# Experts stage: TensorE reads the last 24 row tiles' weight numbers two at a time in twelve steps instead of eight at a time in three

## The chip, the cores and the metric

The kernel runs on one core of one Trainium2 chip. The metric is the device time of the program in microseconds (us), the median of several runs. A core has TensorE (PE in the profile; its weight loads are shown apart, as PEld), VectorE (DVE), ScalarE (ACT), GpSimd (POOL) and SyncE (SP). Each has its own instruction queue, and TensorE's is read by a sequencer that also carries out its waits and register instructions; these are called PEq or PEldq in the profile.

## What is computed

Two blocks of a small transformer, on x of 8 x 1024 rows of 256 numbers. Only the first block's expert part touches the change:

```
xn = layernorm(x)
expert_idx = argmax(xn @ gate_w.T)                 # 8 experts, one for each row
g, u  = xn @ wg[expert], xn @ wu[expert]           # 256 -> 64 each
inter = square(relu(g)) * u
out   = inter @ wd[expert]                         # 64 -> 256
x = x + linear_attention(xn) * silu(out)
xn = layernorm(x)
x = x + block_attention(xn) * silu(layernorm(xn + heads(xn)) * ln_g + ln_b)
```

The kernel leaves out the term `heads(xn)`, the reference's head-wise attention over chosen rows, in both versions; nothing of the second block is touched.

## The kernel before, in words

The program has three parts that follow one another on each engine: `first_layer`, `experts` and `second_layer`. Here only `experts` (from line 1038) matters.

**Sorting.** The first layer scatters the normalised rows into a DRAM table that is sorted by expert. They are then read back as row tiles of 128 rows, each belonging to one expert. There are 72 slots for such tiles (`SLOTS`), worked on in 36 pairs (`PAIRS`), the last with one tile. Which rows stand at which slot is known only at run time: VectorE writes two tables into SBUF, `row_i` (where each tile starts in DRAM) and `owners_i` (the number of the expert whose weights each tile needs, the tile's weight number).

**Registers.** TensorE's matmuls of a tile choose their weights by such a number, which must be in a register of TensorE. It has 48 registers `owners` for this (`OWNERS`), filled by `load_owners` (lines 1210 and 1211), one `TENSOR_LOAD` instruction for eight neighbouring numbers. Six of these loads fill all 48 registers ahead of the stage, between the matmuls of the first layer's last values (`values`, line 1244, with `owners_from`; `whole_values`, line 181, calls `between`). The other 24 numbers follow during the stage, when the first registers are free again: the table `OWNER_LOADS` (line 1047) says in which step.

**The steps.** TensorE's part of the stage is `step(m)` (line 1216), m from 0 to 37, written out without a loop on the chip. In program order a step in the middle of the stage holds:

- `gate_up(m)`: 4 matmuls, `gu_ps`, line 1183, for each a register instruction ahead that works out the address of the weights;
- where `m in OWNER_LOADS`: the load of owners, line 1211;
- `turn_hidden(m - 1)`: 2 transposes, `ht_ps`, line 1193; its first wait is line 1191's, a wait instruction of its own;
- `down(m - 2)`: 4 matmuls, `y_ps`, line 1202, again with a register instruction each;
- `turn(m + 3)`: 4 transposes, `t_ps`, line 1159.

Other engines work on the pairs beside this: ScalarE and VectorE between the matmuls, SP and POOL issue the DMAs that read the row tiles (`load_again`; their own registers `row` are filled from `row_i` by `load_rows`, line 1093, eight at a time) and SP stores `y` to the DRAM tensor `expert_rows`. At the end of the stage POOL waits for all stores (`stored`, ahead of line 1991) and gathers the rows back for the second layer (line 1972).

Before the sorted order is known in full, SP and POOL each take four tile starts one at a time from the same table (`tile_start`, line 223).

Of the kernel before, what the change touches and what calls it, by code (L numbers as in the profile page):

```python
# [39 lines left out]
def program(nc, x, W, gate_w, wg, wu, wd, W_qkv, W_out, b_out, ln_g, ln_b, out):  # L40
# [16 lines left out]
    with ExitStack() as whole:  # L57
# [54 lines left out]
        z.eps_bias = sb("eps_bias", [P, z.D])  # L112
        z.turned = z.wdn[:].rearrange("p e d -> p (e d)").rearrange("p (f k n) -> p f k n", f=4, k=z.KD)
        moe = experts(nc, z, W_qkv, W_out, b_out, ln_g, ln_b)
        second = second_layer(nc, z)
        block = whole.enter_context(nc.Block())
# [64 lines left out]
def whole_values(nc, pe, z, p, banks, free, between=None):  # L181

    v = ORDER[p]
    slot = WHOLE_ROWS.index(v // ROW)
    pe.wait_ge(z.kv_split, WHOLE_ROWS[slot] + 1)
    pe.wait_ge(z.rows_ready, z.UT * free)
    for t in range(z.UT):
        for j in range(z.KD):
            m = nc.tensor.matmul(banks[:, t, 0:z.NV], parked(z, v)[:, j, t * P:(t + 1) * P], z.kvf[:, slot, j, :], start=(j == 0), stop=(j == z.KD - 1))
            if between and j == 0:  # L190
                between(t)
    m.then_inc(z.v_ready, 1)
# [843 lines left out]
def experts(nc, z, W_qkv, W_out, b_out, ln_g, ln_b):  # L1036

    KD, D, E, DE, SLOTS = z.KD, z.D, z.E, z.DE, z.SLOTS
    QUAD = 4
# [3 lines left out]
    PAIRS = SLOTS // 2  # L1043
    ROUNDS = PAIRS // QUAD
    OWNERS, OCTET = 48, 8
    STORE_LAG = 2 * QUAD + 1
    OWNER_LOADS = {14: 48, 17: 56, 20: 64}
    WEIGHT_TURNS = {PAIRS - 3 + f: (f,) for f in range(4)}
    assert PAIRS == ROUNDS * QUAD and OWNERS + OCTET * len(OWNER_LOADS) == SLOTS
    assert z.B * z.L % P == 0  # L1050

    def width(n):

        return 1 if isinstance(n, int) and n == PAIRS - 1 else 2

    with ExitStack() as ctx:
# [90 lines left out]
        def tensor(pe):  # L1147
            def turn(n, i, reused):
                for u in range(2):

                    pe.wait_ge(loaded[u][i], (n - i) * (16 // QUAD) + 16)
                if reused:
                    pe.wait_ge(g["t_copied"], n - 1)
                else:
                    pe.wait_ge(z.first_sems["kv_ready"], ROWS)
                    pe.wait_ge(z.kv_split, ROWS)
                for k in range(KD):
                    for u in range(width(n)):
                        t = nc.tensor.transpose(t_ps[:, i % 2, k, u, :], xg[:, i, u, k * P:(k + 1) * P], z.ident[:])  # L1159
                t.then_inc(g["t_ready"], 1)  # L1160

            def turn_weight(f):

                if f == 0:
                    pe.wait_ge(g["w2_centred"], 3)
                if f < 2:
                    pe.wait_ge(g["t_copied"], PAIRS - 1 + f)
                else:
                    pe.wait_ge(z.turned_copied, f - 1)
                src = z.w2[:, :, f * D:(f + 1) * D] if f < 3 else z.wo[:]  # L1170
                o = t_ps[:, f % 2].rearrange("p k u t -> p k (u t)")
                for k in range(KD):
                    for j in range(KD):
                        t = nc.tensor.transpose(o[:, k, j * P:(j + 1) * P], src[:, j, k * P:(k + 1) * P], z.ident[:])
                t.then_inc(z.turned_ready, 1)

            def gate_up(n, i, e, reused):
                pe.wait_ge(g["t_copied"], n + 1)
                if reused:
                    pe.wait_ge(g["hid_ready"], n - 1)  # L1180
                for u in range(width(n)):
                    for k in range(KD):
                        m = nc.tensor.matmul(gu_ps[:, i % 2, u * 2 * DE:(u + 1) * 2 * DE], xgt[:, i, k, u, :],  # L1183
                                             z.wgu[:, k, bass.ds(e[u], 1), :].rearrange("p a f -> p (a f)"),
                                             start=(u == 0 and k == 0), stop=(k == KD - 1), skip_group_check=True)
                m.then_inc(g["gu_ready"], 1)

            def turn_hidden(n, i, reused):
                pe.wait_ge(g["hid_ready"], n + 1)
                if reused:  # L1190
                    pe.wait_ge(g["ht_copied"], n - 1)
                for u in range(width(n)):
                    t = nc.tensor.transpose(ht_ps[:, i % 2, u * P:(u + 1) * P], hid[:, i % 2, u].rearrange("p c f -> p (c f)"), z.ident[:])
                t.then_inc(g["ht_ready"], 1)

            def down(n, i, e, reused):
                pe.wait_ge(g["ht_copied"], n + 1)
                if reused:
                    pe.wait_ge(g["silu_ready"], n - 1)
                for u in range(width(n)):  # L1200
                    for part in range(2):
                        m = nc.tensor.matmul(y_ps[:, i % 2, u, :], hidt[:, i % 2, u, :],  # L1202
                                             wdn2[:, part, bass.ds(e[u], 1), :].rearrange("p a h -> p (a h)"),
                                             start=(u == 0 and part == 0), stop=(part == 1), skip_group_check=True)
                m.then_inc(g["y_ready"], 1)

            owners = [pe.alloc_register(f"owner{j}") for j in range(OWNERS)]

            def load_owners(first):  # L1210
                pe.load(owners[first % OWNERS:first % OWNERS + OCTET], z.owners_i[0:1, first:first + OCTET])

            def experts_of(n):
                return [pe.snap(owners[(2 * n + u) % OWNERS], min_val=0, max_val=E - 1) for u in range(width(n))]

            def step(m):
                if m < PAIRS:
                    if m == 0:

                        pe.wait_ge(z.rows_ready, z.UT * (START[2] + 1))  # L1220
                    gate_up(m, m % QUAD, experts_of(m), m >= 2)
                if m in OWNER_LOADS:
                    load_owners(OWNER_LOADS[m])
                if m == 0:
                    turn(2, 2, True)
                    values(START[4], START[1])
                    turn(3, 3, True)
                if 1 <= m <= PAIRS:
                    if m == 1:

                        pe.wait_ge(z.rows_ready, z.UT * (START[4] + 1))
                    turn_hidden(m - 1, (m - 1) % QUAD, m - 1 >= 2)
                if m >= 2:
                    if m == 2:

                        pe.wait_ge(z.rows_ready, z.UT * (START[3] + 1))
                        pe.wait_ge(g["wdn_split"], 1)
                    down(m - 2, (m - 2) % QUAD, experts_of(m - 2), m - 2 >= 2)
                if m > 0 and m + 3 < PAIRS:
                    turn(m + 3, (m + 3) % QUAD, True)  # L1240
                for f in WEIGHT_TURNS.get(m, ()):
                    turn_weight(f)

            def values(p, before, owners_from=None):

                load = owners_from is not None and (lambda t: load_owners(owners_from + t * OCTET))
                whole_values(nc, pe, z, p, value_banks[p], before + 1, load)

            values(START[0], TAIL[0])
            pe.wait_ge(z.first_sems["tables_made"], 2)  # L1250
            values(START[1], TAIL[1], 0)
            values(START[2], TAIL[2], 2 * OCTET)
            values(START[3], START[0], 4 * OCTET)
            for i in range(2):
                turn(i, i, False)
            for m in range(PAIRS + 2):
                step(m)
# [785 lines left out]
```

## Time and profile before

| | |
|---|---|
| median of 3 runs | 509.13 us (508.62 to 509.9) |
| profiled execution, its own time | 508.11 us |
| profiled execution, its span | 506.2 us |
| TensorE busy (matmuls) | 494.1 us, 98% of the span |
| VectorE, ScalarE, GpSimd busy | 452.2, 396.5, 320.4 us |
| share of PE in the chain that ended last | 89% |
| loads of owners during the stage | 3, of eight numbers each, at 246.8, 253.5 and 260.2 us |

Times inside a trace count from the span's start. The profiled execution took 1.9 us more than its span; that is what lies before the first and behind the last instruction. Two matmuls that follow one another overlap in the trace, so the pace of TensorE is read from starts, not from durations. Rows for PEldq are instructions that TensorE's sequencer carries out itself; they are not counted as busy time. The step numbers of the stage are found by counting the groups of eight `gu_ps` records: step 14 begins at 246.46 us.

### The profile page before, as it was taken

Reading aid. Unit: us, or ns where it says so; the run is one execution under the profiler, and the core shown is the slowest. Engines: PE = TensorE matmul, PEld = TensorE weight load, DVE = VectorE, ACT = ScalarE, POOL = GpSimd, SP = SyncE. Lnnn points to the kernel's source line nnn. Section 1 sums busy time; section 2 is a strip of 40 time slices with the busy share of each in tenths; the row PEclk is TensorE's granted clock in tenths of the full one; section 3 lists DMA queues with packets and bytes.
Section 4 is the critical chain, followed back from the end, with each engine's and each line's share of the span. In section 5 each row is a group of like instructions: output and inputs, shape, how many; then the busy total and the mean of one; then the engine's idle time right before and its main releaser. Section 6 shows DMA issues by size and latency. Waiting matters only on the chain.

```text
span 506.2 us, 11940 instructions
## 1 busy us (share of the span) xinstructions
PE 494.1 (98%) x3599; PEld 462.9 (91%) x3599; DVE 452.2 (89%) x1428; ACT 396.5 (78%) x910; POOL 320.4 (63%) x377
## 2 busy tenths in 40 slices
PE   6999999999999999999999999999999999999996
PEld 5999999999999999899999998888888898888885
DVE  6999999999999988969889949999999999999975
ACT  4878878787878784378888866788888888888885
POOL 5568876767676877454553028777877777877300
PEclk9999999999999999999999999999999999999999
DMA  7942322222222114558878563265665555655511
GB/s 221 258 126 86 124 84 84 85 84 84 85 85 84 43 53 167 160 170 246 249 231 260 180 206 119 69 145 128 139 147 126 141 131 132 142 139 126 105 42 64
DMA packets 59303, 67.70 MB, mean 134 GB/s; under 512 B 11880, under 2 KB 53616, under 8 KB 59248
## 3 DMA queue, kind: packets, MB, share of 16 engines
q1 hardware_dynamic: 44304, 38.69, 25.5%
q0 software_dynamic: 14944, 28.32, 22.4%
q8 instruction: 29, 0.48, 0.4%
q14 instruction: 26, 0.21, 0.2%
HBM read 39.85 MB, written 27.13 MB: 132 GB/s over the span
## 4 chain that ended last, share of the span: by engine, by line
PE 89%; POOL 3%; DVE 3%; DMA 2%; issue 2%; ACT 1%; SPq 0%; DVEq 0%; POOLq 0%
PE v_ps L1548 10%; PE q_ps L1526 10%; PE gu_ps L1183 6%; PE s_ps L1568 5%; PE y_ps L1202 3%; PE k_ps L171 3%; PE m_ps L171 3%; PE tq_ps L171 3%; PE m_ps L173 3%; PE m_ps L172 3%; PE k_ps L172 3%; PE t_ps L1159 3%; PE k_ps L173 3%; PE tq_ps L172 3%; PE tq_ps L173 3%; PE tq_ps L418 3%
## 5 line engine op out<-in xcount | busy, mean ns | idle before, releaser
L1972 POOL DMA_INDIRECT four<-expert_rows,gather_u x64 | 69.1, 1079 | 37.3 <-DMA expert_rows<-y 18.6
L978 POOL DMA_INDIRECT sorted_rows<-xn,row_u x64 | 67.6, 1057 | 17.2 <-issue 14.1
L967 POOL TENSOR_TENSOR xn<-xn 128x512 fp32r<-128x512 f32 x32 | 43.2, 1350 | 29.6 <-ACT xn L581 29.3
L1526 PE MATMUL q_ps<-xt,wqk 128*128 128x256 f32 x256 | 60.6, 379 | 0.0
L1548 PE MATMUL v_ps<-wvo,xt 128*128 128x256 f32 x248 | 58.7, 379 | 0.0
L1526 PEld LDWEIGHTS q_ps<-xt,wqk 128*128 128x128 f32 x256 | 48.5, 190 | 6.9 <-issue 0.4
L1548 PEld LDWEIGHTS v_ps<-wvo,xt 128*128 128x128 f32 x248 | 44.8, 190 | 4.8
L1978 POOL DMA_DIRECT2D res<-in_L_attn_x x26 | 34.9, 1341 | 19.0 <-DVE res L1775 17.3
L227 POOL DMA_DIRECT2D four<-sorted_rows x36 | 20.0, 555 | 39.8 <-PE t_ps L1159 35.0
L1688 ACT ACTIVATE xn2nd<-res,shift,rstd 128x256 f32<-128x256 f32 (+1 forms) x64 | 34.7, 594 | 7.9 <-DVE shift L1819 7.8
L171 PE MATMUL tq_ps<-xt,wq 128*128 128x256 f32 x128 | 38.4, 300 | 1.9 <-DVE xt L717 1.9
L1987 POOL TENSOR_TENSOR rstd<-var_eps,neg_half 128x4 f32<-128x4 f32 x32 | 35.4, 1106 | 7.7 <-DVE var_eps L1811 7.6
L571 ACT ACTIVATE xn<-four,shift,rstd 128x255 f32<-128x255 f32 x64 | 34.9, 600 | 6.2 <-POOL shift L961 6.2
L609 ACT ACTIVATE k<-kf 128x512 fp32r<-128x512 f32 x32 | 20.2, 630 | 23.7 <-DVE kf L730 23.7
L1183 PE MATMUL gu_ps<-wgu,xgt 128*128 x284 | 37.7, 275 | 0.3 <-ACT xgt L1266 0.3
L171 PE MATMUL k_ps<-wkg,xt 128*128 128x264 f32 x128 | 37.7, 294 | 0.0
L171 PE MATMUL m_ps<-k,xn 128*128 128x256 f32 x128 | 36.2, 283 | 0.4 <-DVE k L736 0.4
L172 PE MATMUL k_ps<-wkg,xt 128*128 128x264 f32 x128 | 36.4, 284 | 0.0
L173 PE MATMUL k_ps<-wkg,xt 128*128 128x264 f32 x128 | 36.3, 283 | 0.0
L173 PE MATMUL m_ps<-k,xn 128*128 128x256 f32 x128 | 36.1, 282 | 0.0
L172 PE MATMUL m_ps<-k,xn 128*128 128x256 f32 x128 | 36.1, 282 | 0.0
L172 PE MATMUL tq_ps<-xt,wq 128*128 128x256 f32 x128 | 35.7, 279 | 0.0
(292 smaller groups left out, 1791.9 us busy)
## 6 DMA issues: line engine op xcount, KB each, us to landing
expert_rows<-y SPq DMA_DIRECT2D x35, 256.0 KB, 3.4
four<-in_L_attn_x SPq DMA_DIRECT2D x32, 256.0 KB, 3.0
out_rows<-att SPq DMA_DIRECT2D x31, 256.0 KB, 2.1
res<-in_L_attn_x POOLq DMA_DIRECT2D x26, 256.0 KB, 4.9
four<-sorted_rows SPq DMA_DIRECT2D x36, 128.0 KB, 3.6
four<-sorted_rows POOLq DMA_DIRECT2D x36, 128.0 KB, 3.3
wdn<-in_L_ffn_wd SPq DMA_DIRECT2D x2, 512.0 KB, 6.8
sorted_rows<-res SPq DMA_DIRECT2D x8, 128.0 KB, 5.7
```

What stands on the lines that cost most here:

```text
L171: nc.tensor.matmul(out, lhs[0], rhs[0], start=first, stop=False, **kw)
L172: nc.tensor.matmul(out, lhs[0], rhs[1], start=False, stop=False, **kw)
L173: return nc.tensor.matmul(out, lhs[1], rhs[0], start=False, stop=last, **kw)
L571: m = nc.scalar.activation(xn[:, i, t, 0:D - 1], xa[:, i % X_SLOTS, t, 0:D - 1], ACT.Identity, bias=shift[:, i % X_SLOTS, t:t + 1], scale= ...
L967: nc.gpsimd.tensor_tensor(xn2[:, s, 1], xn[:, i], xn2[:, s, 0].bitcast(F32), ALU.subtract).then_inc(g["xn_split"], 1)
L978: nc.gpsimd.indirect_dma_start(out=z.sorted_dram.ap(), out_offset=bass.IndirectOffsetOnAxis(ap=row_u[:, i // CU, k:k + 1], axis=0), in_=xn ...
L1183: m = nc.tensor.matmul(gu_ps[:, i % 2, u * 2 * DE:(u + 1) * 2 * DE], xgt[:, i, k, u, :], z.wgu[:, k, bass.ds(e[u], 1), :].rearrange("p a f ...
L1526: m = nc.tensor.matmul(q_ps[:, j, :], wqk[:, k, j * P:(j + 1) * P], xt[:, i % 2, k, :], start=(j == 0 and k == 0), stop=(k == KD - 1), ski ...
L1548: m = nc.tensor.matmul(v_ps[:, t, :], xt[:, i % 2, k, t * P:(t + 1) * P], wvo[:, k, :], start=(t == 0 and k == 0), stop=(k == KD - 1), ski ...
L1972: nc.gpsimd.indirect_dma_start(out=moe[:, n % SLOTS, t, :], out_offset=None, in_=z.expert_dram.ap()[0:(z.SLOTS - 1) * P, :], in_offset=bas ...
L1978: nc.gpsimd.dma_start(tiles(n), x_units[n], accum_op=ALU.add).then_inc(x_added[n % SLOTS], 16)
L1987: nc.gpsimd.tensor_tensor(rstd[:, s], var_eps[:, s], z.neg_half[:, 0:2 * UT].rearrange("p (a t) -> p a t", a=2), ALU.pow).then_inc(g["rstd ...
```

## The change

`OWNER_LOADS` gets twelve entries instead of three: in each of the steps 10 to 21, TensorE reads the weight numbers of one pair of tiles (48 and 49 in step 10, 50 and 51 in step 11, and so on to 70 and 71 in step 21). The six loads of eight ahead of the stage stay as they are.

```diff
     OWNERS, OCTET = 48, 8
     STORE_LAG = 2 * QUAD + 1
-    OWNER_LOADS = {14: 48, 17: 56, 20: 64}
+    OWNER_LOADS = {10 + k: OWNERS + 2 * k for k in range((SLOTS - OWNERS) // 2)}
...
-            def load_owners(first):
-                pe.load(owners[first % OWNERS:first % OWNERS + OCTET], z.owners_i[0:1, first:first + OCTET])
+            def load_owners(first, count):
+                pe.load(owners[first % OWNERS:first % OWNERS + count], z.owners_i[0:1, first:first + count])
...
                 if m in OWNER_LOADS:
-                    load_owners(OWNER_LOADS[m])
+                    load_owners(OWNER_LOADS[m], 2)
...
-                load = owners_from is not None and (lambda t: load_owners(owners_from + t * OCTET))
+                load = owners_from is not None and (lambda t: load_owners(owners_from + t * OCTET, OCTET))
```

TensorE's program in step 10, before the change, from the register instructions of `gate_up` on (ISA is a register instruction, x2 a row that repeats):

```order
L1183 ISA
L1183 MATMUL gu_ps<-wgu,xgt 128x128
L1193 MATMUL ht_ps<-ident,hid 128x128 x2
L1214 ISA
L1202 ISA
```

The same place with the change:

```order
L1183 ISA
L1183 MATMUL gu_ps<-wgu,xgt 128x128
L1211 TENSOR_LOAD owners_i
L1193 MATMUL ht_ps<-ident,hid 128x128 x2
L1214 ISA
L1202 ISA
```

A load stands now between the last matmul of `gate_up` and the first transpose of `turn_hidden`. It stands at the same place in steps 11 to 21; in steps 14, 17 and 20 it stood there before, too. TensorE's program grows by nine instructions, from three loads in the stage to twelve; nothing else on it changes its order, and the programs of the other four engines are the same row for row.

## Rows read from the trace of the kernel before

**Rows 1.** The page, parts 1 and 2: busy time of each engine, TensorE's granted clock

```profile
PE 494.1 (98%) x3599; PEld 462.9 (91%) x3599; DVE 452.2 (89%) x1428; ACT 396.5 (78%) x910; POOL 320.4 (63%) x377
...
PEclk9999999999999999999999999999999999999999
```

**Rows 2.** Timeline of PE: start us, us, engine, line, operation [idle before]

```profile
244.44 1.06 PE L1183 MATMUL gu_ps<-wgu,xgt 128*128 x8
...
246.46 1.06 PE L1183 MATMUL gu_ps<-wgu,xgt 128*128 x8
248.04 0.41 PE L1193 MATMUL ht_ps<-ident,hid 128*128 128x128 f32 x2 [0.53 <-issue]
...
249.44 1.06 PE L1183 MATMUL gu_ps<-wgu,xgt 128*128 x8
...
251.46 1.06 PE L1183 MATMUL gu_ps<-wgu,xgt 128*128 x8
...
253.48 1.06 PE L1183 MATMUL gu_ps<-wgu,xgt 128*128 x8
254.78 0.41 PE L1193 MATMUL ht_ps<-ident,hid 128*128 128x128 f32 x2 [0.24 <-issue]
...
256.13 1.06 PE L1183 MATMUL gu_ps<-wgu,xgt 128*128 x8
...
260.17 1.06 PE L1183 MATMUL gu_ps<-wgu,xgt 128*128 x8
261.47 0.41 PE L1193 MATMUL ht_ps<-ident,hid 128*128 128x128 f32 x2 [0.24 <-issue]
...
262.90 1.06 PE L1183 MATMUL gu_ps<-wgu,xgt 128*128 x8
```

**Rows 3.** TensorE's loads (duration ns min/median/max, starts us): ahead of the stage, then in it

```profile
L1211 PEldq TENSOR_LOAD <-owners_i x6: 588/598/778, 208.6 to 213.1; - x6
...
L1211 PEldq TENSOR_LOAD <-owners_i x3: 1103/1124/1146, 246.8 to 260.2; - x3
```

**Rows 4.** Other engines' loads, the same view: one number each (L223), eight each (L1093)

```profile
L223 SPq TENSOR_LOAD <-row_i x4: 268/316/528, 205.6 to 207.7; - x4
L223 POOLq TENSOR_LOAD <-row_i x4: 286/331/542, 205.6 to 207.7; - x4
...
L1093 POOLq TENSOR_LOAD <-row_i x8: 566/673/906, 211.0 to 271.8; - x8
L1093 SPq TENSOR_LOAD <-row_i x8: 521/536/549, 212.7 to 272.7; - x8
```

**Rows 5.** The wait instruction behind each load and that of the next step: starts

```profile
L1191 PEldq EVENT_SEMAPHORE  x2: 51/51/51, 247.9 to 249.7; - x2
...
L1191 PEldq EVENT_SEMAPHORE  x2: 51/51/51, 254.7 to 256.3; - x2
...
L1191 PEldq EVENT_SEMAPHORE  x2: 51/51/51, 261.4 to 263.1; - x2
```

**Rows 6.** The chain that ended last, 288 to 330 us: start us, us, what

```profile
293.35 0.86 PE y_ps L1202 x4
...
296.08 2.03 DMA expert_rows<-y
...
299.03 1.03 POOL four L1972
...
317.56 3.19 DMA four<-expert_rows,gather_u
...
325.85 0.66 PE t_ps L1539 x4
```

**Rows 7.** Waits, 293 to 330 us: who waited for whom, us, times, longest

```profile
POOL four L1972 <- DMA expert_rows<-y: 18.6, 1, 18.6
```

**Rows 8.** Window of step 14: PE, PEld, DVE, ACT, POOL busy, PEclk, DMA share, GB/s

```profile
246.46:249.44 2.98, 2.45 (x21) 2.15 (x19) 2.61 (x7) 1.99 (x6) 1.21 (x2) 1.00 0.88 233
```

More of the change, by code:

```diff
@@ L1046, in experts @@
     STORE_LAG = 2 * QUAD + 1
-    OWNER_LOADS = {14: 48, 17: 56, 20: 64}
+    OWNER_LOADS = {10 + k: OWNERS + 2 * k for k in range((SLOTS - OWNERS) // 2)}
     WEIGHT_TURNS = {PAIRS - 3 + f: (f,) for f in range(4)}
-    assert PAIRS == ROUNDS * QUAD and OWNERS + OCTET * len(OWNER_LOADS) == SLOTS
+    assert PAIRS == ROUNDS * QUAD and OWNERS + 2 * len(OWNER_LOADS) == SLOTS
     assert z.B * z.L % P == 0
```

## The prediction

> **What bounds the kernel now.** I began with the page's busy times and clock. TensorE is busy for 98% of the span, and its granted clock is in the top tenth in all 40 slices [rows 1]; so what counts is time in which TensorE starts nothing. Next the timeline of TensorE in the experts stage. A step is read from one group of `gu_ps` starts to the next: 244.44 to 246.46, 2.02 us, and the same from 249.44 to 251.46 and on to 253.48 [rows 2]. With no idle time beside it, 2.02 us is the array's own pace. Three steps are longer, and they are the three with a load: 2.98 us (246.46 to 249.44), 2.65 (253.48 to 256.13) and 2.73 (260.17 to 262.90), each with an idle gap ahead of `ht_ps` that is put down to issue [rows 2]. So the three loads cost 0.96 + 0.63 + 0.71 = 2.30 us now, 0.77 each.
>
> Then I asked the loads themselves. Eight numbers took TensorE 0.59 us ahead of the stage, but 1.10 to 1.15 in it, 1.12 in the middle [rows 3]. The sequencer is held that long, while the array works off what was queued before; what the queue does not cover is lost. Last I looked at whether a loss here reaches the end. The chain runs from the last `y_ps` at 293.35 over the store of `y` and POOL's gathers to the second layer's first transposes at 325.85 [rows 6], and POOL had stood waiting for that store for 18.6 us [rows 7]. Nothing in this chain is early, so I pass TensorE's delay on in full.
>
> **The change, part by part.** It removes three loads of eight, puts twelve loads of two in steps 10 to 21, and moves nothing else. Registers are free in time: those that step 10 refills were last used in step 2 and are next read in step 24. SP's, POOL's, ScalarE's and VectorE's programs are the same, and no wait is added; behind the load in TensorE's queue stand `turn_hidden`, `down` and `turn`, and behind these their readers, which all shift with it.
>
> *Removed:* 2.30 us, if all three losses go.
>
> *How long a load of two takes.* No row shows one on TensorE, so I bound it. On SP one number took 0.268 us at least and eight 0.521 at least; on POOL 0.286 and 0.566 [rows 4]. That is (0.521 - 0.268) / 7 = 0.036 us for each further number, 0.040 on POOL. A load is mostly a fixed cost: six numbers fewer save 6 x 0.036 = 0.22 us. Ahead of the stage a load of two would so take 0.59 - 0.22 = 0.37. What doubles the load in the stage (1.12 against 0.59, 0.53 more) the trace doesn't say. SP's loads of eight in the same stage don't show it (0.521 to 0.549), POOL's now and then do (up to 0.906) [rows 4]; it is thus the engine's own doing, not the memory's. The least it can be with two numbers is nothing (0.37), the most that nothing shrinks (1.12). I take a fixed 0.53, since it hardly varies over the three loads, though the first of them came when less was queued (it lost 0.96 where the others lost 0.63 and 0.71): 1.12 - 0.22 = **0.91 us**.
>
> *How fast the sequencer is.* This decides, since twelve loads follow one another, one a step. Behind each of the three loads the array had caught up, and the sequencer ran as fast as it can: from the wait of line 1191 to that of the next step took 249.7 - 247.9 = 1.8, 256.3 - 254.7 = 1.6 and 263.1 - 261.4 = 1.7 us [rows 5], 1.70 in the mean. From a load's end to that wait pass some 0.05 us (260.2 + 1.15 against 261.4 [rows 3, 5]). So a step with no load leaves the sequencer 2.02 - 1.70 = 0.32 us to get ahead, and a step with a load of duration d needs 1.75 + d of sequencer time. With d = 0.91 that is 2.66 us: **0.64 us more than the array's 2.02, in each step**, with nothing to recover it in between.
>
> *The sum.* The first of the twelve meets a sequencer that is ahead, as the three do now: 0.77 - 0.22 = 0.55. The other eleven: 11 x 0.64 = 7.04. Together 7.6 lost, 2.30 given back: **+5.3 us**. The profiled execution took 508.11 us, so 513.4 for one like it; it lay 1.0 us below the median of the three runs (509.13), so I predict a median of **514.4**. The pace of 1.70 is known to about 0.1, which is 1.1 us over eleven steps: 513.3 to 515.5 if the mechanism holds.
>
> For any d the same sum reads: (d - 0.35) + 11 x (d - 0.27) - 2.30. It is zero at d = 0.47. Every rival below but the last is this line with another d.
>
> The Trainium skill, in "DMA: Bandwidth & Descriptors", section "Latency and other measured facts", gives a `tensor_load` floor of about 600 ns. SP's loads of one in 0.268 us [rows 4] lie below that, so the trace speaks against it for SP; it would speak against this change, and no row here tests it for TensorE with fewer than eight.
>
> **The rivals.**
>
> 1. *The count does not matter on TensorE.* Then d = 1.12: 0.77 + 11 x 0.85 - 2.30 = +7.8, 516.9. For it: the cost is mainly fixed on the two other engines. Against it: on both, eight took about twice as long as one [rows 4]. This is where the skill's floor would lead, with the stage's extra on top.
> 2. *The whole load shrinks by one factor.* d = 1.12 / 0.59 x 0.37 = 0.70: 0.35 + 11 x 0.43 - 2.30 = +2.8, 511.9.
> 3. *The stage's extra is a price for each register written.* Then two carry a quarter of it: d = 0.37 + 0.13 = 0.50, 0.15 + 11 x 0.23 - 2.30 = +0.4, 509.5. For it: SP doesn't show the extra, and TensorE alone has register-addressed matmuls queued when it loads. Against it: no row shows such a price.
> 4. *Not slower: short loads hide.* If the extra is gone with so short a load, d = 0.37, and a step needs 1.75 + 0.37 = 2.12 us of the sequencer, 0.10 over the array. 0.02 + 11 x 0.10 - 2.30 = -1.2, 507.9. This decides from d = 0.47 downwards; below 0.34 the gain is over 1.5 us, and it ends at -2.3 (506.8), where all is hidden. For it: six of nine loads on TensorE show no extra. Against it: these six had no register instructions around them, and the three in the stage all show it. The Trainium skill, in "Runtime: NRT & Kernel Launch", section "Instruction fetch mechanics", puts a register load at some 200 ns a register; by that two would take 0.4 and the sum would be -0.8, but eight would take 1.6, and the trace has 0.59 and 1.12 [rows 3].
> **How the numbers follow.** The forecast has 0.47 (513.3 to 515.5), rival 1 0.17, rival 2 0.12, rival 3 0.10, rival 4 0.10, rival 5 0.01; the rest, 0.03, is what I have not thought of. The range goes from rival 4's 507.9 to a little over rival 1's 516.9: 507.8 to 517.2. The cases inside it hold over 0.9, but leaving either out would drop a bound of the unknown duration. A measurement of this kernel tells a change from none at about 0.3%, 1.5 us. Slower by more than that are the forecast and rivals 1, 2 and 5, 0.77 in all, of which I give 0.02 back for a pace of the sequencer that I read too slow: 0.75. Within are rival 3 and most of rival 4: 0.18. Faster by more than 1.5 us, d under 0.34: 0.07.
>
> **What the profile of the changed kernel would show.** Twelve loads in the stage, one in each of steps 10 to 21, of 0.85 to 0.95 us. `gu_ps` groups that start 2.6 to 2.75 us apart from step 11 on, with an idle gap of about 0.4 us put down to issue ahead of every `ht_ps`, and 2.02 again from step 22. The wait of line 1191 comes 1.75 us plus a load behind the one before. The last `y_ps` of the stage and the second layer's first transposes both come 5 us later, and behind 330 us nothing is longer than before. I am wrong if a load of two takes under 0.6 or over 1.05 us, if the steps with loads stay near 2.02, or if TensorE's delay at 293 us isn't found again at 326.

## The result, and the profile after

Measured side by side on one chip, the change takes 512.92 us (median of 4 runs, 512.62 to 513.2) and the kernel before 509.51 (4 runs, 508.62 to 510.06): a ratio of 1.0066, 95% interval 1.0048 to 1.0083. It is slower by 3.4 us, 2.4 to 4.2 by the interval. The profiled execution took 513.1 us, its span 511.2.

Busy time and granted clock, parts 1 and 2 of the page of the changed kernel, to set against [rows 1]:

```profile
PE 499.0 (98%) x3599; PEld 465.4 (91%) x3599; DVE 452.9 (89%) x1428; ACT 396.5 (78%) x910; POOL 320.8 (63%) x377
...
PEclk9899999999999999999999999999999999999999
```

PE's busy time grew by 4.9 us with the same 3599 matmuls, and the others' stayed. Most of that lies in the changed steps. Windows over steps 10 to 21, before and after (us; PE, PEld, DVE, ACT, POOL busy; PEclk, DMA share, GB/s):

```profile
238.37:264.92 26.55, 25.54 (x219) 24.60 (x217) 22.56 (x53) 23.16 (x60) 14.31 (x19) 1.00 0.82 243
...
240.44:269.72 29.28, 28.86 (x219) 25.50 (x217) 23.11 (x54) 23.67 (x60) 14.69 (x19) 1.00 0.77 223
```

The twelve steps take 2.73 us more, and TensorE is recorded as busy for 3.3 us more, so the loss doesn't look like idle time. Without a load, `ht_ps` starts 0.89 us behind `gu_ps`, whose group of records lasts 1.06: the two overlap. With a load it starts 1.04 us behind, the overlap is gone, and the lost time counts as busy. A busy share can't show this loss; starts can.

The clock's second slice is a tenth lower. It lies over 200 us ahead of the first changed instruction and is not the change's. The changed kernel's stage also began late in this execution, ahead of any changed instruction; whether the clock is the reason isn't shown, but it has to be taken off first. First and last starts of three kinds of matmul (duration ns min/median/max, first and last start us), in the kernel before:

```profile
L1159 PE MATMUL t_ps<-ident,four x142: 270/272/274, 214.4 to 286.8; 128*128 128x128 f32 x142
L1202 PE MATMUL y_ps<-wdn,hidt x142: 277/284/384, 222.4 to 294.6; 128*128 x142
L1539 PE MATMUL t_ps<-ident,xn2nd x128: 272/274/328, 310.9 to 491.0; 128*128 128x128 f32 x64, 128*127 128x128 f32 x64
```

The same rows of the changed kernel:

```profile
L1159 PE MATMUL t_ps<-ident,four x142: 270/272/329, 216.3 to 291.6; 128*128 128x128 f32 x142
L1202 PE MATMUL y_ps<-wdn,hidt x142: 277/288/388, 224.3 to 299.4; 128*128 x142
L1539 PE MATMUL t_ps<-ident,xn2nd x128: 272/274/329, 316.9 to 496.0; 128*128 128x128 f32 x64, 128*127 128x128 f32 x64
```

The stage began 1.9 us late (216.3 against 214.4) and ended 4.8 us late (299.4 against 294.6). So the stage itself gave 2.9 us, and the last transpose of the second layer is 5.0 us late, as the span is. The group that started at 325.85 in the chain of [rows 6] is 5.25 us late (timeline of PE of the changed kernel):

```profile
331.10 0.65 PE L1539 MATMUL t_ps<-ident,xn2nd 128*128 128x128 f32 x4
```

Between the two parts the lateness is not constant: the second layer's very first transposes are 6.0 us late (316.9 against 310.9). The wait that [rows 7] showed for the store of `y` is unchanged, in the waits of GpSimd (who waited for whom, us, times, longest):

```profile
POOL four L1972 <- DMA expert_rows<-y: 18.5, 1, 18.5
```

TensorE's steps, timeline of PE of the changed kernel (start us, us):

```profile
238.29 1.06 PE L1183 MATMUL gu_ps<-wgu,xgt 128*128 x8
...
240.44 1.06 PE L1183 MATMUL gu_ps<-wgu,xgt 128*128 x8
241.48 0.41 PE L1193 MATMUL ht_ps<-ident,hid 128*128 128x128 f32 x2
...
242.83 1.06 PE L1183 MATMUL gu_ps<-wgu,xgt 128*128 x8
244.03 0.41 PE L1193 MATMUL ht_ps<-ident,hid 128*128 128x128 f32 x2
...
245.40 1.06 PE L1183 MATMUL gu_ps<-wgu,xgt 128*128 x8
...
269.72 1.06 PE L1183 MATMUL gu_ps<-wgu,xgt 128*128 x8
270.61 0.38 PE L1193 MATMUL ht_ps<-ident,hid 128*128 128x128 f32 x2
...
271.74 1.06 PE L1183 MATMUL gu_ps<-wgu,xgt 128*128 x8
```

Step 10 starts at 240.44, step 22 at 269.72: 29.28 us for twelve steps, 2.44 each, where the array's own pace is 24.24 (12 x 2.02). In the kernel before, the same twelve took 26.55. From step 22 on it is 2.02 again (269.72 to 271.74). `ht_ps` starts 1.04 and 1.20 us behind `gu_ps` in the first two steps with a load, 0.89 in the first without.

TensorE's loads in the stage, then the first three alone, then the wait of line 1191 over steps 10 to 21 (same columns as above), of the changed kernel:

```profile
L1211 PEldq TENSOR_LOAD <-owners_i x12: 533/628/818, 240.7 to 267.5; - x12
...
L1211 PEldq TENSOR_LOAD <-owners_i x1: 590/590/590, 240.7 to 240.7; - x1
...
L1211 PEldq TENSOR_LOAD <-owners_i x1: 818/818/818, 243.0 to 243.0; - x1
...
L1211 PEldq TENSOR_LOAD <-owners_i x1: 550/550/550, 245.6 to 245.6; - x1
...
L1191 PEldq EVENT_SEMAPHORE  x12: 51/51/51, 241.4 to 268.2; - x12
```

The twelve loads have a mean of 0.654 us, against the 1.12 of [rows 3]. The waits come (268.2 - 241.4) / 11 = 2.44 us apart; less 0.65 that leaves 1.78, where I had 1.75. The later kernels with a load in every step give the same: 2.33 us between loads less a mean of 0.54 is 1.79 in twos_turn, 2.31 less a mean of 0.51 is 1.80 in ones24.

### The profile page after: what moved, and what is told of

Read it like the earlier page. It is cut to its first block, busy times and chain, and to the rows that moved or that the text cites. A ratio compares the mean times of both kernels' runs of the same rounds, so it can differ in the third digit from the quotient of the medians.

```text
span 511.2 us, 11949 instructions
## 1 busy us (share of the span) xinstructions
PE 499.0 (98%) x3599; PEld 465.4 (91%) x3599; DVE 452.9 (89%) x1428; ACT 396.5 (78%) x910; POOL 320.8 (63%) x377
## 4 chain that ended last, share of the span: by engine, by line
PE 90%; issue 2%; DVE 2%; DMA 2%; SPq 1%; ACT 1%; POOL 1%; DVEq 0%; another core or an unknown queue 0%
PE q_ps L1526 11%; PE v_ps L1548 10%; PE gu_ps L1183 6%; PE s_ps L1568 6%; PE y_ps L1202 4%; PE k_ps L171 3%; PE k_ps L173 3%; PE k_ps L172 3%; PE t_ps L1159 3%; PE tq_ps L171 3%; PE tq_ps L172 3%; PE tq_ps L173 3%; PE t_ps L1539 3%; PE m_ps L171 3%; PE m_ps L173 3%; PE a_ps L1579 3%
## 5 line engine op out<-in xcount | busy, mean ns | idle before, releaser
L171 PE MATMUL k_ps<-wkg,xt 128*128 128x264 f32 x128 | 38.2, 298 | 0.0
L172 PE MATMUL k_ps<-wkg,xt 128*128 128x264 f32 x128 | 36.8, 288 | 0.0
L173 PE MATMUL k_ps<-wkg,xt 128*128 128x264 f32 x128 | 36.6, 286 | 0.0
```

The source lines that it names most:

```text
L171: nc.tensor.matmul(out, lhs[0], rhs[0], start=first, stop=False, **kw)
L172: nc.tensor.matmul(out, lhs[0], rhs[1], start=False, stop=False, **kw)
L173: return nc.tensor.matmul(out, lhs[1], rhs[0], start=False, stop=last, **kw)
```

## The experiments

Two questions stayed open: how long a load takes and why, and whether TensorE's delay reaches the end. Each kernel below is an edit of one of the two kernels. "Stage" is the time from the first `gu_ps` of step 3 to that of step 33; it is 63.44 us in the kernel before and 66.37 with the change. The stages are from one profiled execution each; all ratios are to the kernel before on the same chip, with their 95% interval.

| kernel | ratio | stage, against before |
|---|---|---|
| the change | 1.0066 [1.0048, 1.0083] | +2.9 us |
| no_loads | 0.9979 [0.9965, 0.9994] | -2.0 |
| eights9 | 1.0170 [1.0148, 1.0192] | +10.1 |
| ones24 | 1.0094 [1.0077, 1.0111] | +4.2 |
| twos_apart | 1.0096 [1.0079, 1.0113] | +3.3 |
| one24 | 1.0004 [0.9990, 1.0018] | -0.7 |
| eights_turn | 0.9991 [0.9980, 1.0003] | -0.8 |
| twos_turn | 1.0048 [1.0032, 1.0064] | +1.6 |
| eights_off2 | 1.0091 [1.0067, 1.0114] | +5.3 |
| fours_gate | 0.9979 [0.9963, 0.9995] | -1.7 |
| fours_turn | 0.9981 [0.9971, 0.9991] | -1.1 |
| eights_end | 0.9993 [0.9983, 1.0004] | -0.7 |

**No loads in the stage.** From the kernel before:

```diff
-    OWNER_LOADS = {14: 48, 17: 56, 20: 64}
+    OWNER_LOADS = {}
```

> The stage without any load of owners; it leaves out that the last 24 row tiles get their own weight numbers (they are worked with those of the first 24). All theories: the 2.30 us read from the three long steps of the kernel before come back, so 2.3 us faster than before, steps 14, 17 and 20 at 2.02 us, and the shift is found again at the end. If the loss did not reach the end, it would be less than 1 us faster.

Measured: 506.71 us against 507.55. The last `y_ps` and the last transpose of the second layer:

```profile
L1202 PE MATMUL y_ps<-wdn,hidt x142: 277/283/384, 222.8 to 292.9; 128*128 x142
...
L1539 PE MATMUL t_ps<-ident,xn2nd x128: 272/274/329, 309.3 to 489.6; 128*128 128x128 f32 x64, 128*127 128x128 f32 x64
```

The stage is 2.0 us shorter, near the 2.30 that the three loads were said to cost. The runs gained 0.8 us, 0.3 to 1.8 by the interval, so the profiled stage's gain lies a little above it. By the change's own numbers (stage +2.9, runs 2.4 to 4.2) the delay is passed on in full. The passage from the stage to the second layer can give or take some 1 us, though: in the traces of twos_apart and ones24 the last `y_ps` is 5.4 and 6.2 us later than before, the last transpose of the second layer only 4.4 and 5.2.

**Nine loads of eight, twos' places.** From the change: the load of step 10 + k starts at 48 + 2k as there, but reads eight, and there are nine of them, in steps 10 to 18; the last reads 64 to 71.

```diff
-    OWNER_LOADS = {10 + k: OWNERS + 2 * k for k in range((SLOTS - OWNERS) // 2)}
+    OWNER_LOADS = {10 + k: OWNERS + 2 * k for k in range(9)}
...
-                    load_owners(OWNER_LOADS[m], 2)
+                    load_owners(OWNER_LOADS[m], OCTET)
```

> Nine loads of eight in steps 10 to 18, each advancing by two numbers (the same numbers end in the same registers). Theory 1, the length of a load in the stage goes by how many numbers it reads (1.12 us for eight, 0.65 in the mean for the two of the change, so some 0.08 a number): all nine take 1.1 us, the steps after the first some 2.87 us, and the kernel is 0.77 + 8 x 0.85 - 2.30 = 5.3 us slower than before. Theory 2, the extra in the stage comes from how much array work stands queued when the load begins, which is much less when every step has a load: the first takes 1.1 us, the others some 0.8, steps of 2.55 us, and it is 0.77 + 8 x 0.53 - 2.30 = 2.7 us slower than before.

The loads of steps 10 to 13, starting at numbers 48, 50, 52 and 54:

```profile
L1211 PEldq TENSOR_LOAD <-owners_i x1: 1002/1002/1002, 239.7 to 239.7; - x1
...
L1211 PEldq TENSOR_LOAD <-owners_i x1: 2322/2322/2322, 242.5 to 242.5; - x1
...
L1211 PEldq TENSOR_LOAD <-owners_i x1: 593/593/593, 246.6 to 246.6; - x1
...
L1211 PEldq TENSOR_LOAD <-owners_i x1: 2628/2628/2628, 248.9 to 248.9; - x1
```

No theory of mine had this: they gave the kernel 5.3 or 2.7 us more than before, and the runs have some 9. Of the nine loads, those that start at a multiple of four take 0.59 (the first 1.00), those between take 2.3 to 2.6. All loads of the kernel before start at multiples of eight.

The granted clock also fell here. Windows of steps 11 to 14 (us; PE, PEld, DVE, ACT, POOL busy; PEclk, DMA share, GB/s):

```profile
242.33:246.39 4.06, 2.43 (x20) 2.10 (x19) 1.83 (x4) 1.99 (x6) 1.82 (x2) 1.00 0.68 210
246.39:248.74 2.35, 2.35 (x20) 2.12 (x19) 1.60 (x4) 1.99 (x6) 0.55 (x1) 1.00 0.33 77
248.74:253.74 5.00, 3.02 (x21) 2.63 (x20) 2.27 (x6) 2.35 (x6) 1.83 (x2) 0.89 0.56 177
253.74:256.86 3.12, 3.12 (x20) 3.12 (x19) 1.52 (x4) 1.80 (x5) 0.56 (x1) 0.63 0.52 159
```

So its +10.1 us is not the loads' alone: step 14, with a load of 0.59, took 3.12 us at a mean of 0.63 where step 12 took 2.35 at 1.00. The profiled execution was the slowest of four (518.62 us, median 516.60).

**One number a step, in 23 steps.** From the change.

```diff
-    OWNER_LOADS = {10 + k: OWNERS + 2 * k for k in range((SLOTS - OWNERS) // 2)}
+    OWNER_LOADS = {10 + k: OWNERS + k for k in range(SLOTS - OWNERS)}
...
-                    load_owners(OWNER_LOADS[m], 2)
+                    load_owners(OWNER_LOADS[m], 1)
```

> One number a step, in steps 10 to 32 (23 loads, the last number is never read). Theory 1 (by the count): a load of one takes 0.58 us, steps of 2.33 us, 0.23 + 22 x 0.31 - 2.30 = 4.7 us slower than before. Theory 2 (by the queue): a load of one takes 0.04 less than the change's of two, 0.62 us, and it is 0.27 + 22 x 0.35 - 2.30 = 5.7 us slower. Both: slower than the change, since the number of loads counts more than their size.

```profile
L1211 PEldq TENSOR_LOAD <-owners_i x23: 304/541/736, 240.6 to 291.3; - x23
```

The table has 24 entries and the trace 23 loads, since the last pair has one tile only. A single number can be had in 0.30 us, half of the eight's 0.59 and little over half of the two's 0.53. There is no floor at 0.6 on this engine. The Trainium skill's ("DMA: Bandwidth & Descriptors", "Latency and other measured facts": about 600 ns) is what an aligned eight takes here, not the least. Other loads of one number reach up to 0.74, so something is added while the count stays the same. The runs are 5.2 us slower than before, between the two theories' 4.7 and 5.7, though a load had a mean of 0.51 us and not 0.58 or 0.62.

**Twos with a free step between them** (steps 3, 5, ... 25). From the change.

```diff
-    OWNER_LOADS = {10 + k: OWNERS + 2 * k for k in range((SLOTS - OWNERS) // 2)}
+    OWNER_LOADS = {3 + 2 * k: OWNERS + 2 * k for k in range((SLOTS - OWNERS) // 2)}
```

> The change's twelve loads of two in every other step, 3 to 25, so that the sequencer is ahead again before each. Theory 1 (by the count): a load takes 0.65 us as in the change and costs 0.77 - (1.12 - 0.65) = 0.3 us, 12 x 0.3 - 2.30 = 1.3 us slower than before. Theory 2 (by the queue): with the queue full again each takes 0.9 us and costs 0.55, 12 x 0.55 - 2.30 = 4.3 us slower.

The first load, and the eleven behind it:

```profile
L1211 PEldq TENSOR_LOAD <-owners_i x1: 544/544/544, 225.8 to 225.8; - x1
...
L1211 PEldq TENSOR_LOAD <-owners_i x11: 816/1059/1162, 229.8 to 275.7; - x11
```

The same instruction takes 0.54 or 1.06. With a free step in between the extra of some 0.5 is there in ten of twelve, as large as in [rows 3]; with a load in each step it is 0.28 at most. This kernel is no faster than the change for its free steps. Its runs are 5.1 us slower than before, near the 4.3 of theory 2, while its stage is 3.3 us longer; what the rest is, the runs don't show.

**All 24 in one load, in step 17.** From the kernel before, `OWNER_LOADS` has one entry, and the load reads 48 to 71 into registers 0 to 23 at once.

```diff
-    OWNER_LOADS = {14: 48, 17: 56, 20: 64}
+    OWNER_LOADS = {17: 48}
...
-                    load_owners(OWNER_LOADS[m])
+                    pe.load(owners[0:24], z.owners_i[0:1, 48:72])
```

> All 24 numbers by a single load in step 17, instead of three of eight. An isolated load of two costs 0.55 us in the runs so far, one of eight 0.77, so some 0.037 a number. Queue theory (a load in the stage waits until the array has nearly run out of what was queued ahead of it, and then takes its reading time): 0.77 + 16 x 0.037 = 1.4 us, against 2.3 for the three: 0.9 us faster than before, and a load of some 1.7 us. If every number carries a share of the stage's extra (0.53 / 8 = 0.066 besides 0.037), the load takes 2.8 us and the three are only replaced by one as dear: no change.

```profile
L1223 PEldq TENSOR_LOAD <-owners_i x1: 2114/2114/2114, 253.6 to 253.6; - x1
```

The stage gains 0.7 us in the trace; the runs can't tell it from before. Six reads of four, at 0.33 for the first and 0.26 (0.59 - 0.33, by the later runs) for each further one, make 1.63 us. That leaves 0.5, the size of one extra: by this reckoning, from one load, the extra comes once a load, not once a register. One for each register would have made it 2.8 us.

**The same loads behind `down`, ahead of `turn`.** From the kernel before (eights_turn) and from the change (twos_turn, with `load_owners(OWNER_LOADS[m], 2)`):

```diff
-                if m in OWNER_LOADS:
-                    load_owners(OWNER_LOADS[m])
...
                     down(m - 2, (m - 2) % QUAD, experts_of(m - 2), m - 2 >= 2)
+                if m in OWNER_LOADS:
+                    load_owners(OWNER_LOADS[m])
```

> The three loads of eight stand behind down's matmuls, ahead of the transposes of turn, instead of behind gate_up's; there only some 0.3 us of array work is queued ahead of the load, and what follows it is work that the sequencer hands out quickly. Queue theory: the load takes 0.6 to 0.7 us and costs 0.4 us, 3 x 0.4 - 2.30 = 1.1 us faster than before. Fixed extra (0.53 us wherever a load of the stage stands): 1.1 us a load, 0.9 us lost each, 0.4 us slower than before.

```profile
L1211 PEldq TENSOR_LOAD <-owners_i x3: 596/596/598, 249.6 to 262.7; - x3
```

> The change with its twelve loads of two at that same place, behind down. Queue theory: 0.40 to 0.45 us each, steps of 2.2 us, 12 x 0.18 - 2.30: within 0.5 us of the kernel before. Fixed extra: 0.9 us each, steps of 2.65 us, 5 us slower than before. In either case the steps still go by the sequencer's time, 1.75 us plus the load.

```profile
L1211 PEldq TENSOR_LOAD <-owners_i x12: 532/538/578, 241.8 to 267.4; - x12
```

Here the extra is gone from all fifteen loads, and what is left is the load itself: 0.60 for eight, 0.54 for two. Two numbers cost almost what eight do. The runs can't tell eights_turn from before. twos_turn is slower than before by 2.5 us (512.35 against 509.86), since 12 x 0.54 = 6.5 us of the sequencer stands against 3 x 1.12 = 3.4 in the kernel before, where free steps followed each load besides. The lengths come nearest to the queue theory, but a two was to take 0.40 to 0.45 by it.

**Eights at even, unaligned starts, and a two alone.** From the change; four loads, in steps 11, 14, 17 and 20.

```diff
-    OWNER_LOADS = {10 + k: OWNERS + 2 * k for k in range((SLOTS - OWNERS) // 2)}
+    OWNER_LOADS = {11: (48, 2), 14: (50, 8), 17: (58, 8), 20: (66, 6)}
...
-                    load_owners(OWNER_LOADS[m], 2)
+                    load_owners(*OWNER_LOADS[m])
```

> The loads of steps 14, 17 and 20 begin two numbers later (50 with eight, 58 with eight, 66 with six), and a load of two in step 11 reads 48 and 49. It asks why every second of the nine loads of eight took 2.3 to 2.6 us in the run before: those began at 50, 54, 58 and 62. If it is where in the table a load of eight begins, the loads of steps 14 and 17 take 2.3 us again and the kernel is some 3 us slower than before. If it came from the rhythm of one load a step, they take 1.1 us as in the kernel before, and the kernel is 0.4 us slower (one more isolated load of two, two numbers fewer).

The load of two, the first of the two loads of eight, and the load of six:

```profile
L1211 PEldq TENSOR_LOAD <-owners_i x1: 1104/1104/1104, 242.7 to 242.7; - x1
...
L1211 PEldq TENSOR_LOAD <-owners_i x1: 2473/2473/2473, 249.7 to 249.7; - x1
...
L1211 PEldq TENSOR_LOAD <-owners_i x1: 1831/1831/1831, 266.9 to 266.9; - x1
```

Where the load starts decides: in step 14, eight numbers from 50 take 2.47 us, from 48 they took 1.1. With eights9's 2.32 for eight and ones24's 0.30 for one, a further number costs (2.32 - 0.30) / 7 = 0.29 us where the load isn't aligned. If the aligned four inside 50 to 57 were still taken as one, it would be five reads, some 1.5 us. The Trainium skill's figure of some 200 ns a register ("Runtime: NRT & Kernel Launch", "Instruction fetch mechanics"), which that page gives for the runtime's own loads, fits neither kind here: 0.29 us a number unaligned, 0.59 / 8 = 0.07 aligned.

The kernel is some 5 us slower in the runs, where 3 was expected. Part of its stage's +5.3 is the clock again. Windows of step 14, with the load from 50, and of step 15 (columns as above):

```profile
249.44:253.89 4.45, 2.61 (x21) 2.30 (x19) 2.51 (x7) 2.20 (x6) 1.11 (x2) 0.95 0.72 230
253.89:257.32 3.43, 3.43 (x19) 3.43 (x19) 1.79 (x4) 1.96 (x6) 1.83 (x2) 0.56 0.50 153
```

Step 15 has no load and took 3.43 us at a mean of 0.56.

**Six aligned fours,** in steps 10, 12, ... 20, behind `gate_up` (fours_gate) or behind `down` (fours_turn, where the load also moves as in twos_turn). From the change:

```diff
-    OWNER_LOADS = {10 + k: OWNERS + 2 * k for k in range((SLOTS - OWNERS) // 2)}
+    OWNER_LOADS = {10 + 2 * k: OWNERS + 4 * k for k in range((SLOTS - OWNERS) // 4)}
...
-                    load_owners(OWNER_LOADS[m], 2)
+                    load_owners(OWNER_LOADS[m], 4)
```

> Six loads of four in steps 10, 12, ... 20, behind gate_up as in the change, each beginning at a multiple of four. Block theory (TensorE's load makes one read of 0.27 to 0.29 us for each aligned block of four numbers it wants in full, and one for each single number otherwise; eight aligned: two reads, 0.59; eight begun two later: eight reads, 2.3; two: two reads, 0.54): a load of four is one read, 0.29 plus a wait of up to 0.5, 0.8 us at most, and costs some 0.3: 6 x 0.3 - 2.30 = 0.5 us faster than before. Count theory (each number is a read of 0.27, eight aligned alone is dealt with faster): 1.1 plus the wait, 1.1 us lost each, 4 us slower than before.

```profile
L1211 PEldq TENSOR_LOAD <-owners_i x6: 335/414/714, 240.0 to 260.5; - x6
```

> The same six loads of four behind down, where loads of eight took 0.60 us and cost 0.46 each and showed no wait. Block theory: 0.30 us a load, 0.46 - 0.30 = 0.16 us lost, 6 x 0.16 - 2.30 = 1.3 us faster than before: the best of all tried. Count theory: 1.1 us a load, 0.95 lost, 3.4 us slower than before.

```profile
L1211 PEldq TENSOR_LOAD <-owners_i x6: 332/336/520, 241.1 to 262.1; - x6
```

Four aligned numbers take 0.33 us, less than two (0.53) and hardly more than one (0.30): an aligned block of four is read at once, as the block theory had it; by the count theory it would take 1.1. Both kernels are faster than before, 508.81 and 508.99 against 510.08 us. They have the lowest ratios of the kernels that compute the whole, the same as no_loads has; against the change it is about 0.9%, through the two ratios (0.9979 / 1.0066 = 0.991) and not side by side. They lie within each other's intervals, and those of eights_turn and eights_end overlap theirs. Behind `gate_up` the first three took 0.34 us each, the other three 0.71, 0.49 and 0.51: an extra is there again, without a free step more or less. Behind `down` the last of the six shows one, 0.52 against 0.33.

**Eights at the very end of a step, behind `turn`:** the edit of eights_turn, with the two lines behind `turn(m + 3, ...)`.

> The kernel before with its three loads of eight at the end of the step, behind turn's four transposes, so that some 0.7 us of array work is queued ahead, of which the last 0.44 us are transposes, whose operands no register chooses. It asks what the extra 0.5 us behind gate_up is. Queue theory (the load waits for whatever array work is queued ahead): 0.9 to 1.0 us a load, about as dear as before. Register theory (it waits only for queued matmuls whose weights a register chose): 0.60 us a load, 0.3 us lost or less each, 1.5 us faster than before.

```profile
L1211 PEldq TENSOR_LOAD <-owners_i x2: 597/597/597, 248.5 to 255.1; - x2
...
L1211 PEldq TENSOR_LOAD <-owners_i x1: 904/904/904, 261.5 to 261.5; - x1
```

Two of the three show no extra and one 0.31. Neither theory has this: one said 0.9 to 1.0 us for each, the other 0.60 for each. The runs can't tell it from before.

## Why the prediction was right

514.4 us was forecast, with 507.8 to 517.2 around it and 0.75 on slower. 512.92 lies inside, on the side forecast and 1.5 us below the forecast itself. As a difference it is +3.4 us against a forecast of +5.3. The mechanism was right, a sequencer that can't keep up once each step has a load; one term of the sum, the length of a load, was not. Point by point:

- *Removed, 2.30 us:* held nearly. Without the loads the stage is 2.0 us shorter.
- *The sequencer needs 1.75 + d in a step with a load, nothing recovers it in between:* held. 2.44 us a step with a mean d of 0.654, which makes it 1.78 + d, and 1.79 and 1.80 in two other kernels; steps at 2.02 again once the loads end. This is why it is slower although each load is far shorter than those it replaces.
- *The whole delay reaches the end:* held for the change, +2.9 in the stage and 2.4 to 4.2 in the runs. twos_apart and ones24 lost some 1 us of their delay between the stage and the second layer, so this is known to about 1 us. For no_loads the runs gave less than the stage (0.3 to 1.8 against 2.0), so for a gain it is not shown to be in full.
- *The length of a load, d = 0.91:* this is the term that was mis-sized; it measured 0.654. With it my own line gives 0.30 + 11 x 0.384 - 2.30 = +2.2 us, against +2.7 over steps 10 to 21 and +2.9 over the stage. Two parts of d were wrong, in opposite directions. The reading: I took 0.036 us for each further number from SP's one and eight [rows 4] and had 0.37 for two. It is 0.53, because the slope isn't one: eight aligned numbers are two reads of four, and two numbers are two reads as well. The extra: I took it as a fixed 0.53 in every load, since it hardly varied over three. It was 0 to 0.28 in the twelve, 0.12 in the mean (0.654 - 0.535). I had three samples from one situation, loads three steps apart, and carried them over to another. [rows 3] held a warning: of the six loads ahead of the stage one took 0.78 us where the others took some 0.6. So an extra of another size was on show, and five of nine loads, not the six that rival 4 counts, were without one. That the time came out within 1.5 us is partly luck: a reading 0.16 us too short offset part of an extra 0.41 us too long, and the kernel before measured 0.4 us higher beside the change (509.51) than in the runs that the forecast started from (509.13). With the measured d the same line gives 511.4 us.
- *Signs in the profile:* loads of 0.85 to 0.95 and steps of 2.6 to 2.75 us were wrong with d. The idle gap of 0.4 us ahead of each `ht_ps` didn't show either: groups of records no longer overlapped, and the loss counts in TensorE's busy time. The steps did return to 2.02, the last `y_ps` and the group at 326 did come some 5 us later. A load of two under 0.6 us was named as a sign of being wrong: six of the twelve are under it, the mean of 0.654 is not.
- *Rivals:* rival 2's d of 0.70 lies nearest to the measured mean, and its 511.9 us is nearer to 512.92 than the forecast is, but for the wrong reason. Rivals 1 and 3 fail too: no factor, floor or price per register describes loads of 0.30, 0.33, 0.53, 0.59 and 2.32 us for one, four, two, eight and eight numbers. Rival 4, that short loads hide, comes nearest with the aligned fours: 1.75 + 0.33 is 2.08 us, 0.06 over the array's 2.02, and the free step behind it has 0.32 to recover that. In fours_gate three of the six steps with a load took 2.02 to 2.03 us and the others 2.17 to 2.32. Rival 5, the clock, was not met by the change.

**What stays open** is what the extra waits for. It comes once a load by the reckoning from one24, behind `gate_up` in most loads where a free step came before (ten of twelve in twos_apart), in none of three early fours in the same situation, and behind `down` in one of 21 (0.19 us). In the change the first eight loads alternate, 0.59, 0.82, 0.55, 0.76, 0.57, 0.77, 0.56, 0.75 us, so what the step before did may matter, which is not shown. I tried place and spacing; neither gives a clean rule. Nor was it tried to give TensorE more than 48 registers, which would do away with some of the loads.

## What to carry to other kernels

When an instruction stream is held by its sequencer, count instructions and their time on the sequencer per step, not the numbers they carry. Three long stalls with free steps between them can cost less than twelve short ones that each exceed the slack of a step. Where registers are loaded in small portions, try aligned blocks of four: here they gave the least time a step, 0.33 us a load. And a price taken as a slope between two sizes needs a third size before it is used.

## What the runs showed of the hardware that I had not expected

- A `TENSOR_LOAD` on TensorE: 0.30 us for one number, 0.53 for two, 0.33 for four aligned, 0.59 for eight aligned, 2.3 to 2.6 for eight that start two past a multiple of four. SP's 0.268 for one and 0.521 for eight [rows 4] fit the same count of reads, one and two.
- The same load can take about 0.5 us more or not, by what stands around it.
- A long sequencer stall can be followed by a lower clock. In eights9 the load of 2.32 us in step 11 left the granted clock at 1.00; with the one of 2.63 in step 13 the windows of steps 13 and 14 show 0.89 and 0.63, that is time at the 1.2 GHz level. eights_off2's first load of 2.47 us was followed by 0.56, its second of 2.49 and one24's of 2.11 by no fall. The length of the load alone doesn't tell: TensorE had been idle for 1.93 and 1.84 us ahead of `ht_ps` in the two cases with a fall, for 1.63, 1.00 and 1.20 us in the three without. In the change, with its short stalls, it stayed at 1.00 in the stage.
